# Expert slots of a two-layer mixture-of-experts kernel: gate and up products taken with the weights as the stationary operand

## The chip, the cores and the metric

One core of a Trainium2 chip runs the whole program. The metric is the device time of one execution, in microseconds; lower is better.

## The reference, cut to what matters

Two layers work on x of 16 x 256 tokens with 128 features. Each layer is: normalise and modulate, attention, residual, normalise and modulate, mixture of experts, residual. Only the mixture of experts is touched here. For each token one expert is chosen by the largest router logit; its feed-forward is added to that of a shared expert. Layer 0 (8 experts, hidden width 256) and layer 1 (7 experts, one of the 8 router outputs standing for "none", hidden width 512):

```
h = silu(x_ @ gate[e].T) * (x_ @ up[e].T)          # layer 0, e = argmax of the logits
y = h @ down[e].T                                  # plus the shared expert, same form
hid = (x @ up_w[e]) * silu(x @ gate_w[e])          # layer 1
routed = hid @ down_w[e]                           # 0 where the chosen index is 7
out = ALPHA * top1_val * routed + shared
```

All matrices are fp32.

## The kernel before, in words

The kernel keeps X (features on the partitions, tokens along the row) in SBUF and runs the stages one after the other. In the mixture stage (function `moe`, one on each engine) the tokens are sorted by expert: VectorE works out a place for each token, GpSimd scatters 32 tiles of 128 token rows to the HBM tensor `sorted_rows` (L1458), meanwhile TensorE does the shared expert (L534, L536, L543). Every expert's run of rows is padded to a multiple of 128, so that 39 slots of 128 rows (SLOTS) hold all tokens, each slot of one expert. `eid` holds for each slot the first column of its expert in the weight tensors.

The slots are a software pipeline over k, 39 in each layer:

- SyncE, `tiles` (L259 to L268): waits for all scatters (L261), then fetches slot k's rows, 128 rows of 130 floats, into a ring of 12 places (L268). From k = 12 on it waits for the slot 12 back to be turned, weighted and sent.
- TensorE, loop at L609: `gate_up(k)` (L578, L582), then the register load `first_column(k + 1)` (L564, 4 bytes of `eid` into a TensorE register), `turn(k + 2)` (L571, transpose of the rows), `turn_hidden(k - 1)` (L591, 2 transposes in layer 0, 4 in layer 1), `sum_down(k - 2)` (L600, 2 or 4 products into one bank). In `gate_up` the token block is stationary and the expert's weights are the moving operand, 256 or 512 columns, read from the SBUF copies of all experts at a column held in a register. The product has tokens on the partitions and so has to be turned before `sum_down`.
- ScalarE: `copy_x` (L881) takes the turned rows from PSUM, `silu` (L888) the gate, `weight` (L895) scales the finished slot into `slot_out`.
- VectorE: `gate_hidden` (L1272) multiplies the silu of gate by up, `copy_hidden` (L1280) takes the turned product from PSUM.
- GpSimd: `send` (L1464) scatters the slot's rows to the HBM tensor `token_rows`.

Each engine carries out its list in order, with semaphores between them. After the slots SyncE (`returned`) waits for the sends (12 waits, L275) and fetches the rows back in 8 transfers (L277); TensorE turns them (L628) and VectorE adds them to X (L1157). In layer 0 SyncE also fetches layer 1's up weights, 2 MB, right behind its last slot transfer (L282).

Every fp32 product is two passes, so L578 and L582 appear as x2 for each slot, and L600 as x4 (layer 0) or x8 (layer 1); the transposes are one pass each.

Of the kernel before, what the change touches and what calls it, by code (L numbers as in the profile page):

```python
# [40 lines left out]
def adaln_kernel(nc, a):  # L41
    ctx = ExitStack()
    with ctx:
# [86 lines left out]
        pw = sb("pw", [P, 2, 4, 3 * P])  # L130
        zb = sb("zb", [P, 2 * HEADS1 * DEPTH])
# [51 lines left out]
        slot_sems = {n: sem("r_" + n) for n in ("xt_even", "xt_odd", "eid", "xk", "xf", "gate", "up", "silu", "hidden", "ht", "hf", "down", "y")}  # L183
        r_load, r_sent = [sem(f"r_load{n}") for n in range(RING)], [sem(f"r_sent{n}") for n in range(RING)]
        for l in range(2):
            RS[l].update(slot_sems, load=r_load, sent=r_sent)
# [28 lines left out]
        def of_slot(l, k):  # L215

            return 16 * (l * LOADS[k % RING] + k // RING + 1)

# [3 lines left out]
        def _(sp):  # L222
# [36 lines left out]
            def tiles(l):  # L259
                q = RS[l]  # L260
                sp.wait_ge(q["dispatched"], 16 * TILES)  # L261
                for k in range(SLOTS):
# [5 lines left out]
                    sp.dma_start(slot_in[:, r, :], sorted_rows[l][k * P:(k + 1) * P, :]).then_inc(q["load"][r], 16)  # L268

# [23 lines left out]
        def _(pe):  # L293
# [210 lines left out]
            def moe(c):  # L504
                E, NH, HID, l = c["E"], c["NH"], c["HID"], c["l"]
                up, gate, down, q = c["up"], c["gate"], c["down"], RS[c["l"]]
                up_f = up.rearrange("p e h -> p (e h)")
                gate_f = gate.rearrange("p e h -> p (e h)")
# [76 lines left out]
                def turn_hidden(k):  # L585
                    b = k % 2
                    pe.wait_ge(q["hidden"], l * SLOTS + k + 1)
                    if k >= 2:
                        pe.wait_ge(q["hf"], l * SLOTS + k - 1)
                    for n in range(NH):  # L590
                        m = nc.tensor.transpose(PS[:, 4 + b, n * P:(n + 1) * P], rsb[:, b, n * P:(n + 1) * P], ident[:, :])  # L591
                    m.then_inc(q["ht"], 1)
# [153 lines left out]
        def _(act):  # L746
# [113 lines left out]
            def moe(c):  # L860
# [39 lines left out]
                for k in range(SLOTS + 2):  # L900
                    if k < SLOTS:
                        silu(k)
                    if k + 2 < SLOTS:
                        copy_x(k + 2)
# [650 lines left out]
```

## Time and profile before

| | |
|---|---|
| three runs | 1098.90, 1098.04, 1094.33 us, median 1098.04 |
| profiled execution | 1097.04 us, its span 1095.3 us |
| mean granted TensorE clock | 0.942 |
| TensorE busy | 89% of the span; VectorE 58%, ScalarE 50%, GpSimd 41% |
| slots of layer 0 | from about 605 to 675 us of the span |
| slots of layer 1 | from about 950 to 1080 us of the span |

Times in the rows are us from the start of the span, durations in us unless marked ns. PE is TensorE's matrix multiply, PEld its weight load (which runs beside it), PEldq its sequencer's register work, SPq SyncE's issuing of DMAs. A busy PE is a modelled figure: matmuls are pipelined, and the distance between two starts says more than one duration. A granted clock of 1.00 is 2.4 GHz, 0.50 is 1.2 GHz.

### The profile page before, as it was taken

Reading aid. Unit: us, or ns where it says so; the run is one execution under the profiler, and the core shown is the slowest. Engines: PE = TensorE matmul, PEld = TensorE weight load, DVE = VectorE, ACT = ScalarE, POOL = GpSimd, SP = SyncE. Lnnn points to the kernel's source line nnn. Section 1 sums busy time; section 2 is a strip of 40 time slices with the busy share of each in tenths; the row PEclk is TensorE's granted clock in tenths of the full one; section 3 lists DMA queues with packets and bytes.
Section 4 is the critical chain, followed back from the end, with each engine's and each line's share of the span. In section 5 each row is a group of like instructions: output and inputs, shape, how many; then the busy total and the mean of one; then the engine's idle time right before and its main releaser. Section 6 shows DMA issues by size and latency. Waiting matters only on the chain.

```text
span 1095.3 us, 20328 instructions
## 1 busy us (share of the span) xinstructions
PE 976.8 (89%) x6976; PEld 586.4 (54%) x6976; DVE 632.1 (58%) x2018; ACT 547.5 (50%) x1080; POOL 450.0 (41%) x681
## 2 busy tenths in 40 slices
PE   7778999999986989699889997799997999999995
PEld 4356666666662332244444796356654644366664
DVE  2558888888833789622454343667763633343443
ACT  4605666666666545544622563557775422234331
POOL 1116667766740799200037354035541073023221
PEclk9859999999998998899989998889998899999998
DMA  6500000000002000300001335000000012011105
GB/s 215 193 0 2 2 3 2 3 2 3 2 2 86 1 0 1 153 1 0 1 24 52 78 82 181 8 1 2 1 2 1 1 51 57 0 38 44 43 28 165
DMA packets 31873, 41.91 MB, mean 38 GB/s; under 512 B 6880, under 2 KB 26720, under 8 KB 30912
## 3 DMA queue, kind: packets, MB, share of 16 engines
q1 hardware_dynamic: 27232, 31.26, 9.2%
q0 software_dynamic: 4544, 9.38, 2.6%
q8 instruction: 58, 0.95, 0.4%
q14 instruction: 39, 0.32, 0.1%
HBM read 29.16 MB, written 16.66 MB: 42 GB/s over the span
## 4 chain that ended last, share of the span: by engine, by line
PE 46%; ACT 3%; POOL 3%; DVE 3%; issue 3%; DMA 2%; SPq 0%; DVEq 0%; POOLq 0%
PE PS L578 5%; PE PS L600 5%; PE PS L582 5%; PE PS L534 3%; POOL sorted_rows L1458 3%; PE PS L495 3%; PE PS L536 3%; PE PS L543 3%; PE PS L500 3%; PE PS L591 2%; PE PS L301 2%; PE PS L682 2%; PE PS L701 2%; PE PS L669 2%; PE PS L712 2%
## 5 line engine op out<-in xcount | busy, mean ns | idle before, releaser
L804 ACT ACTIVATE pw<-PS 128x384 f32<-128x384 f32 x256 | 111.7, 488 | 79.1 <-PE PS L415 77.0
L1401 POOL TENSOR_SCALAR_AFFINE_SELECT pw<-pw 128x256 f32<-128x256 f32 x256 | 104.2, 431 | 96.2 <-ACT pw L804 94.3
L1035 DVE CUSTOM_DVE_ANT_0 PS<-PS,above 128x256 f32<-128x256 f32 x256 | 115.3, 450 | 47.2 <-PE PS L390 45.3
L1464 POOL DMA_INDIRECT token_rows<-xnb,slot_in x78 | 74.5, 955 | 161.4 <-ACT xnb L895 161.4
L393 PE MATMUL PS<-kf,qm 32*128 32x256 f32 x512 | 96.4, 454 | 13.2 <-DVE mx L1037 8.0
L1272 DVE TENSOR_TENSOR rsb<-sqb,PS 128x256 f32<-128x256 f32 (+1 forms) x78 | 43.3, 555 | 112.4 <-ACT sqb L888 99.0
L1451 POOL TENSOR_TENSOR XS<-XS,N 128x512 f32<-128x512 f32 x64 | 80.1, 1290 | 28.1 <-DVE N L1108 24.4
L1423 POOL TENSOR_SCALAR_AFFINE_SELECT pw<-pw 128x256 f32<-128x256 f32 x128 | 55.7, 469 | 71.9 <-ACT pw L925 71.9
L1037 DVE CUSTOM_DVE_ANT_0 PS<-PS,above 128x128 f32<-128x128 f32 x256 | 84.4, 330 | 0.0
L1410 POOL TENSOR_SCALAR qm<-qs,qmask 128x256 f32<-128x256 f32 x64 | 60.0, 939 | 56.1 <-ACT kf L790 56.1
L418 PE MATMUL PS<-qm,kf 32*128 32x256 f32 x512 | 82.8, 400 | 0.0
L1458 POOL DMA_INDIRECT sorted_rows<-H,pos x32 | 30.8, 964 | 126.1 <-DVE pos L1253 116.7
L877 ACT ACTIVATE sqb<-PS 128x512 f32<-128x512 f32 x48 | 28.7, 597 | 96.7 <-PE PS L534 96.7
L1010 DVE TENSOR_TENSOR xnb<-PS,rsb 128x512 f32<-128x512 f32 x56 | 38.7, 691 | 65.0 <-ACT rsb L770 45.0
L1183 DVE TENSOR_TENSOR rsb<-sqb,PS 128x512 f32<-128x512 f32 x48 | 32.8, 686 | 68.9 <-PE PS L536 68.9
L483 PE MATMUL PS<-N,wxs 128*128 128x512 f32 x112 | 63.3, 663 | 6.1 <-DVE N L1117 3.3
L846 ACT ACTIVATE PS<-PS,cols 128x512 f32<-128x512 f32 x64 | 42.4, 662 | 41.7 <-DVE N L1117 22.8
L925 ACT ACTIVATE pw<-PS 128x768 f32<-128x768 f32 x64 | 48.4, 809 | 23.4 <-PE PS L685 23.4
L895 ACT ACTIVATE xnb<-PS,slot_in 128x128 f32<-128x128 f32 x78 | 28.6, 367 | 59.8 <-PE PS L600 59.8
L310 PE MATMUL PS<-sqb,meanm 128*128 128x512 f32 x112 | 57.8, 604 | 0.6 <-ACT sqb L759 0.5
L759 ACT ACTIVATE sqb<-PS 128x512 f32<-128x512 f32 x56 | 33.1, 593 | 49.6 <-PE PS L301 47.3
L435 PE MATMUL PS<-pw,region 128*32 128x256 f32 (+1 forms) x1024 | 54.9, 332 | 1.0 <-POOL pw L1401 1.0
(206 smaller groups left out, 2382.8 us busy)
## 6 DMA issues: line engine op xcount, KB each, us to landing
sorted_rows<-empty_rows_dram SPq DMA_DIRECT2D x2, 2535.0 KB, 14.9
slot_in<-sorted_rows SPq DMA_DIRECT2D x78, 65.0 KB, 1.9
N<-token_rows SPq DMA_DIRECT2D x16, 256.0 KB, 4.9
X<-xT_dram SPq DMA_DIRECT2D x4, 512.0 KB, 6.9
ATT<-gate_dram SPq DMA_DIRECT2D x1, 2048.0 KB, 7.7
XS<-down_dram SPq DMA_DIRECT2D x1, 2048.0 KB, 12.3
H<-up_dram SPq DMA_DIRECT2D x1, 2048.0 KB, 8.3
out_dram<-X SPq DMA_DIRECT2D x8, 256.0 KB, 3.3
```

The lines of the kernel that those rows point to most:

```text
L310: nc.tensor.matmul(PS[:, LN_PSV + k % 2, :], meanm[:, :], sqb[:, k % 4, :], start=True, stop=True).then_inc(ln_var, 1)
L393: m = nc.tensor.matmul(PS[:, bank, 0:SEQ], qm[r, b % 3, g, P:SEQ], kf[r, b % 3, :], start=True, stop=True)
L418: m = nc.tensor.matmul(PS[:, bank, 0:SEQ], kf[r, b % 3, 0:P], qm[r, b % 3, g, :], start=False, stop=True, skip_group_check=True)
L483: nc.tensor.matmul(PS[:, k, :], wxs[:, :], V[:, s], start=False, stop=True, skip_group_check=True).then_inc(i_p, 1)
L804: nc.scalar.activation(pw[:, w % 2, j + n, :], PS[:, A_PST + (2 * v + n) % 3, 0:3 * P], ACT.Exp).then_inc(a_p, 1)
L1035: nc.vector.tensor_tensor_reduce(x[:, 0:SEQ], x[:, 0:SEQ], above[:, :], 1.0, -3e38, ALU.add, ALU.max, mx[:, 1, j, g:g + 1])
L1037: nc.vector.tensor_tensor_reduce(x[:, SEQ:SEQ + P], x[:, SEQ:SEQ + P], above[:, P:SEQ], 1.0, -3e38, ALU.add, ALU.max, mx[:, 0, j, g:g + 1] ...
L1401: m = nc.gpsimd.affine_select(x[:, :, SEQ * k:SEQ * k + P], x[:, :, SEQ * k:SEQ * k + P], [[0, 2], [1, P]], ALU.is_ge, 0.0, base=0, channe ...
L1410: nc.gpsimd.tensor_scalar(qm[:, b % 3, g, :], qs[:, b % 2, :], qmask[:, g:g + 1], None, ALU.mult).then_inc(a_q, 1)
L1451: nc.gpsimd.tensor_tensor(XS[:, s], XS[:, s], V[:, s], ALU.add).then_inc(i_x, 1)
L1458: nc.gpsimd.indirect_dma_start(sorted_rows[l][:, :], bass.IndirectOffsetOnAxis(pos[:, n:n + 1], 0), rows[l][:, n, :], None).then_inc(q["di ...
L1464: nc.gpsimd.indirect_dma_start(token_rows[l][:, :], bass.IndirectOffsetOnAxis(slot_in[:, r, D:D + 1].bitcast(mybir.dt.int32), 0), slot_out ...
```

## The change

In the slots, `gate_up` takes the weights as the stationary operand, 128 columns at a time, and the block of 128 tokens as the moving operand. The product comes out with the hidden units on the partitions, as `sum_down` wants it: `turn_hidden`, `copy_hidden` and their semaphores are gone, and the loop on TensorE is one step shorter. Each slot's gate and up weights (2 x 128 KB in layer 0, 2 x 256 KB in layer 1) no longer come from the resident copies: SyncE loads the slot's column from `eid` into a register of its own and transfers both blocks from HBM to one of two fixed places for each. The resident copies stay, for the shared expert. `copy_x` moves from ScalarE to VectorE.

```diff
+        wgate, wup = [pw[:, :, :, :].rearrange("p w u t -> p (w u t)")[:, 2 * FF * n:2 * FF * (n + 1)]
+                      .rearrange("p (b h) -> p b h", b=2) for n in range(2)]
...
+        def of_weights(l, k):
+            return 16 * (l * ((SLOTS + 1 - k % 2) // 2) + k // 2 + 1)
...
             def tiles(l):
                 q = RS[l]
-                sp.wait_ge(q["dispatched"], 16 * TILES)
-                for k in range(SLOTS):
+                HID, cap = MOE[l]["HID"], MOE[l]["cap"]
+                gate_f, up_f = [a[f"{n}{l}"].rearrange("p e h -> p (e h)") for n in ("gate", "up")]
+
+                def rows_in(k):
                     r = k % RING
                     if k >= RING:
                         sp.wait_ge(q["xk"], l * SLOTS + k - RING + 1)
                         sp.wait_ge(q["y"], l * SLOTS + k - RING + 1)
                         sp.wait_ge(q["sent"][r], of_slot(l, k - RING))
                     sp.dma_start(slot_in[:, r, :], sorted_rows[l][k * P:(k + 1) * P, :]).then_inc(q["load"][r], 16)
+
+                def weights_in(k):
+                    e = sp.value_load(eid[0:1, k:k + 1], min_val=0, max_val=cap * HID)
+                    if k >= 2:
+                        sp.wait_ge(q["gate"], l * SLOTS + k - 1)
+                    sp.dma_start(wgate[:, k % 2, 0:HID], gate_f[:, bass.ds(e, HID)]).then_inc(q["wgate"][k % 2], 16)
+                    if k >= 2:
+                        sp.wait_ge(q["up"], l * SLOTS + k - 1)
+                    sp.dma_start(wup[:, k % 2, 0:HID], up_f[:, bass.ds(e, HID)]).then_inc(q["wup"][k % 2], 16)
+
+                sp.wait_ge(q["eid"], l + 1)
+                for k in range(2):
+                    weights_in(k)
+                sp.wait_ge(q["dispatched"], 16 * TILES)
+                for k in range(OUTS):
+                    rows_in(k)
+                for k in range(SLOTS):
+                    if k + 2 < SLOTS:
+                        weights_in(k + 2)
+                    if k + OUTS < SLOTS:
+                        rows_in(k + OUTS)
...
-                def gate_up(k, e):
+                def gate_up(k):
                     b = k % 2
                     pe.wait_ge(q["xf"], l * SLOTS + k + 1)
+                    pe.wait_ge(q["wgate"][b], of_weights(l, k))
                     if k >= 2:
                         pe.wait_ge(q["silu"], l * SLOTS + k - 1)
-                    nc.tensor.matmul(PS[:, b, 0:HID], xnb[:, b, 0:P], gate_f[:, bass.ds(e, HID)],
-                                     start=True, stop=True).then_inc(q["gate"], 1)
+                    for n in range(NH):
+                        m = nc.tensor.matmul(PS[:, b, n * P:(n + 1) * P], wgate[:, b, n * P:(n + 1) * P], xnb[:, b, 0:P],
+                                             start=True, stop=True)
+                    m.then_inc(q["gate"], 1)
+                    pe.wait_ge(q["wup"][b], of_weights(l, k))
                     if k >= 2:
                         pe.wait_ge(q["hidden"], l * SLOTS + k - 1)
-                    nc.tensor.matmul(PS[:, 2 + b, 0:HID], xnb[:, b, 0:P], up_f[:, bass.ds(e, HID)],
-                                     start=True, stop=True).then_inc(q["up"], 1)
+                    for n in range(NH):
+                        m = nc.tensor.matmul(PS[:, 2 + b, n * P:(n + 1) * P], wup[:, b, n * P:(n + 1) * P], xnb[:, b, 0:P],
+                                             start=True, stop=True)
+                    m.then_inc(q["up"], 1)
...
                 def sum_down(k, e):
                     b = k % 2
-                    pe.wait_ge(q["hf"], l * SLOTS + k + 1)
+                    pe.wait_ge(q["hidden"], l * SLOTS + k + 1)
                     if k:
                         pe.wait_ge(q["y"], l * SLOTS + k)
                     for n in range(NH):
-                        m = nc.tensor.matmul(PS[:, 6, 0:D], rsb[:, 2 + b, n * P:(n + 1) * P],
+                        m = nc.tensor.matmul(PS[:, 6, 0:D], rsb[:, b, n * P:(n + 1) * P],
                                              down_f[:, bass.ds(e + n * D, D)], start=(n == 0), stop=(n == NH - 1))
...
-                for k in range(SLOTS + 2):
+                for k in range(SLOTS + 1):
                     if k < SLOTS:
-                        gate_up(k, columns[k])
+                        gate_up(k)
                     if k + 1 < SLOTS:
                         columns[k + 1] = first_column(k + 1)
                     if k + 2 < SLOTS:
                         turn(k + 2)
-                    if 1 <= k <= SLOTS:
-                        turn_hidden(k - 1)
-                    if k >= 2:
-                        sum_down(k - 2, columns[k - 2])
+                    if k:
+                        sum_down(k - 1, columns[k - 1])
...
+                copy_x(0)
+                copy_x(1)
+                for k in range(SLOTS):
+                    gate_hidden(k)
+                    if k + 2 < SLOTS:
+                        copy_x(k + 2)
```

The last lines are VectorE's loop after the change; ScalarE's keeps `silu(k)` and `weight(k - 1)`. SyncE's loop issues three transfers for each slot in place of one, and the slots' rows run 8 ahead in place of 12.

## Rows read from the trace of the kernel before

**Rows 1.** Page, part 1: busy time, share of the span, instructions of each engine.
```profile
PE 976.8 (89%) x6976; PEld 586.4 (54%) x6976; DVE 632.1 (58%) x2018; ACT 547.5 (50%) x1080; POOL 450.0 (41%) x681
```
**Rows 2.** Windows: stretch, then busy PE, PEld, DVE, ACT, POOL; clock, DMA share, GB/s.
```profile
612.00:640.00 28.00, 28.00 (x190) 25.41 (x189) 12.97 (x35) 17.47 (x51) 16.27 (x17) 1.00 0.28 75
1000.00:1060.00 60.00, 60.00 (x326) 40.90 (x325) 24.50 (x38) 23.59 (x57) 18.09 (x19) 1.00 0.15 40
```
**Rows 3.** Chain of waits, one slot of layer 0: start, us, what.
```profile
641.64 0.43 PE PS L578 x2
642.08 0.43 PE PS L582 x2
642.51 0.11 PE PS L571
642.62 0.22 PE PS L591 x2
642.84 0.45 PE PS L600 x4
```
**Rows 4.** Chain of waits, one slot of layer 1.
```profile
1000.03 0.44 PE PS L591 x4
1000.47 0.89 PE PS L600 x8
1001.36 0.86 PE PS L578 x2
1002.22 0.86 PE PS L582 x2
1003.08 0.11 PE PS L571
```
**Rows 5.** Groups of instructions between 1000 and 1060 us, layer 1's slots.
```profile
L600 PEld LDWEIGHTS PS<-XS,rsb 128*128 128x128 f32 x152 | 18.5, 192 | 0.0
L1280 DVE COPY rsb<-PS 128x512 f32<-128x512 f32 x19 | 13.0, 684 | 0.0
```
**Rows 6.** SyncE: timeline from 603.5 us; L268's issues (min/median/max ns); DMA to landing.
```profile
603.59 5.55 SPq L268 DMA_DIRECT2D slot_in<-sorted_rows  x12
L268 SPq DMA_DIRECT2D slot_in<-sorted_rows x78: 319/320/1319, 603.6 to 1045.4; - x78
w<-w_dram SPq DMA_DIRECT2D x2, 256.0 KB, 2.9
wctx<-wctx_dram SPq DMA_DIRECT2D x1, 64.0 KB, 1.9
```
**Rows 7.** Timeline, start of layer 1's slots: start, us, engine, line [idle before].
```profile
948.52 0.88 DVE L1157 SCALAR_TENSOR_TENSOR X<-PS,gab,X 128x256 f32<-128x256 f32 x2 [1.22 <-PE PS L543]
950.19 0.14 PEld L571 LDWEIGHTS PS<-ident,slot_in 128*128 128x128 f32 x1 [2.54 <-issue]
950.56 0.28 ACT L881 ACTIVATE xnb<-PS 128x128 f32<-128x128 f32 x1 [4.28 <-PE PS L571]
950.95 0.14 PEld L571 LDWEIGHTS PS<-ident,slot_in 128*128 128x128 f32 x1 [0.62 <-issue]
```
**Rows 8.** L578's register instructions (min/median/max ns).
```profile
L578 PEldq FUSED_REGOPS  x78: 37/44/46, 606.2 to 1068.8; - x78
```
**Rows 9.** Ends of both slot stages: last up product, last send, SyncE's next issue.
```profile
669.69 0.59 PE L582 MATMUL PS<-region,xnb 128*128 x2
674.27 2.24 DMA token_rows<-xnb,slot_in
676.69 5.71 SPq L277 DMA_DIRECT2D N<-token_rows  x8
1071.43 1.02 PE L582 MATMUL PS<-H,xnb 128*128 x2
1078.00 2.22 DMA token_rows<-xnb,slot_in
```
**Rows 10.** L1464, all sends: issue to landing; layer 0's sends as a group.
```profile
DMA to landing us min/median/max: 2.2/2.4/6.7
L1464 POOL DMA_INDIRECT token_rows<-xnb,slot_in x39 | 37.3, 957 | 35.8 <-ACT xnb L895 35.8
```
**Rows 11.** Windows, columns as in rows 2: two stretches in which TensorE waits.
```profile
50.00:60.00 10.00, 5.79 (x28) 4.38 (x30) 4.11 (x24) 0.37 (x2) 3.63 (x4) 0.50 0.00 1
350.00:360.00 10.00, 6.68 (x16) 2.60 (x15) 5.99 (x11) 6.58 (x11) 0.01 (x1) 1.00 0.00 0
```

More of the change, by code:

```diff
@@ L182, in adaln_kernel @@
             "back", "x")} for l in range(2)]
-        slot_sems = {n: sem("r_" + n) for n in ("xt_even", "xt_odd", "eid", "xk", "xf", "gate", "up", "silu", "hidden", "ht", "hf", "down", "y")}
+        slot_sems = {n: sem("r_" + n) for n in ("xt_even", "xt_odd", "eid", "xk", "xf", "gate", "up", "silu", "hidden", "down", "y")}
+        r_wgate, r_wup = [sem(f"r_wgate{n}") for n in range(2)], [sem(f"r_wup{n}") for n in range(2)]
         r_load, r_sent = [sem(f"r_load{n}") for n in range(RING)], [sem(f"r_sent{n}") for n in range(RING)]
         for l in range(2):
-            RS[l].update(slot_sems, load=r_load, sent=r_sent)
+            RS[l].update(slot_sems, load=r_load, sent=r_sent, wgate=r_wgate, wup=r_wup)
         r_rows = [sem(f"r_rows{n}") for n in range(NCH)]
@@ L506, in moe @@
                 up, gate, down, q = c["up"], c["gate"], c["down"], RS[c["l"]]
-                up_f = up.rearrange("p e h -> p (e h)")
-                gate_f = gate.rearrange("p e h -> p (e h)")
                 down_f = (down[:, :, :, :] if l == 0 else down).rearrange("p e j d -> p (e j d)")
@@ L615, in moe @@
                         turn(k + 2)
-                    if 1 <= k <= SLOTS:
-                        turn_hidden(k - 1)
-                    if k >= 2:
-                        sum_down(k - 2, columns[k - 2])
+                    if k:
+                        sum_down(k - 1, columns[k - 1])
             def turn_back(l, k):
@@ L877, in moe @@
                     nc.scalar.activation(sqb[:, j % 2, :], PS[:, j % 2, :], ACT.Silu).then_inc(q["s_silu"], 1)
-                def copy_x(k):
-                    act.wait_ge(q["xk"], l * SLOTS + k + 1)
-                    nc.scalar.activation(xnb[:, k % 2, 0:P], PS[:, 7, 0:P], ACT.Copy).then_inc(q["xf"], 1)
                 def silu(k):
@@ L896, in weight @@
                                          scale=slot_in[:, r, D + 1:D + 2]).then_inc(q["y"], 1)
-                copy_x(0)
-                copy_x(1)
-                for k in range(SLOTS + 2):
+                for k in range(SLOTS + 1):
                     if k < SLOTS:
                         silu(k)
-                    if k + 2 < SLOTS:
-                        copy_x(k + 2)
-                    if k >= 2:
-                        weight(k - 2)
+                    if k:
+                        weight(k - 1)
             nc.scalar.preload_act_table_set(LN_EXP)
@@ L1270, in gate_hidden, with copy_x @@
                     if k >= 2:
-                        dve.wait_ge(q["ht"], l * SLOTS + k - 1)
+                        dve.wait_ge(q["down"], l * SLOTS + k - 1)
                     nc.vector.tensor_tensor(rsb[:, b, 0:HID], sqb[:, b, 0:HID], PS[:, 2 + b, 0:HID],
                                             ALU.mult).then_inc(q["hidden"], 1)
-                def copy_hidden(k):
-                    b = k % 2
-                    dve.wait_ge(q["ht"], l * SLOTS + k + 1)
-                    if k >= 2:
-                        dve.wait_ge(q["down"], l * SLOTS + k - 1)
-                    nc.vector.tensor_copy(rsb[:, 2 + b, 0:HID], PS[:, 4 + b, 0:HID]).then_inc(q["hf"], 1)
-                for k in range(SLOTS + 1):
-                    if k < SLOTS:
-                        gate_hidden(k)
-                    if k:
-                        copy_hidden(k - 1)
+                def copy_x(k):
+                    dve.wait_ge(q["xk"], l * SLOTS + k + 1)
+                    nc.vector.tensor_copy(xnb[:, k % 2, 0:P], PS[:, 7, 0:P]).then_inc(q["xf"], 1)
+                copy_x(0)
[4 more added lines that the diff above has]
+                        copy_x(k + 2)
             def add_routed(l, k):
```

8 lines of the change are left out of this document (1 added, 7 removed).

## The prediction

> **What bounds the kernel now.** I read the page first: TensorE is busy for 89% of the span [rows 1], but that is a mean over many stages, so the two slot stages are read by themselves. The windows inside them [rows 2] show TensorE busy without a break at full clock (28.00 of 28.00 us, 60.00 of 60.00), every other engine under two thirds busy, and the DMA engines at a share of 0.28 and 0.15. The chain of waits consists there of TensorE alone [rows 3, 4], and its pieces are the price list. Layer 0: gate 0.43, up 0.43, turn 0.11, two transposes 0.22, down 0.45, together 1.64 us a slot. Layer 1: 0.86 + 0.86 + 0.11 + 0.44 + 0.89 = 3.16 us a slot. So each TensorE instruction saved in a slot is saved from the time, until something else ends last. SyncE issues one DMA a slot and is idle otherwise; nothing of the old profile warns of it, and it is where the change puts its work.
>
> **TensorE.** New gate and up are of down's kind: a 128x128 fp32 stationary block, 128 columns moving, two passes. Eight such passes take 0.89 us [rows 4], four 0.45 [rows 3]. Layer 1: three times 0.89 + 0.11 = 2.78 in place of 3.16, 0.38 less. Layer 0: three times 0.45 + 0.11 = 1.46 in place of 1.64, 0.18 less. The two transposed steps' waits on VectorE vanish with them. What must hold is that weight loads go beside products: each of down's loads takes 192 ns by itself [rows 5], and yet eight loads and eight passes fit in 0.89 us, 0.11 for a pair. The Trainium skill, page "TensorE: Matmul & The Clock Gate", section "The mechanism", says that a weight load overlaps a running product only where the two use different row groups. By that rule the pair would cost load plus pass; the rows of down contradict it for just this shape.
>
> **VectorE and ScalarE.** VectorE loses a copy of 256 or 512 columns (0.68 us for 512 [rows 5]) and takes one of 128, surely less; ScalarE loses one. Both were covered by TensorE and have more room now. I cost them at nothing in the steady state. GpSimd needs 0.96 us a send [rows 10] against at least 1.46 a slot: covered.
>
> **Layer 1's sum.** Up to the last up product 37 slots' transposes go (37 x 0.44 = 16.3), 78 products grow by 0.03 (2.3), and one more down stands ahead of it, since the lag is a step shorter (0.9): -13.1. The tail: before, 5.7 us from the end of the last up product (1071.43 + 0.86) to the last send's issue at 1078.00 [rows 9]. After: product on VectorE 0.69, down 0.89, weighting 0.37, four hand-offs of about 0.15: 2.6. So -3.1. Layer 1 together: -16, if SyncE and the DMAs keep up.
>
> **Do they in layer 1?** Gate's place for slot k+2 is free when gate(k) ends, and is needed when gate(k+2) starts, two slots less one gate later: 5.56 - 0.89 = 4.7 us. A 256 KB transfer lands 2.9 us after its issue [rows 6]; with hand-offs 3.2. There is 1.5 us of room. Data: two blocks of 256 KB and the rows come to some 640 KB in 2.8 us, 230 GB/s; the 256 KB landing 1.0 us later than a 64 KB one (2.9 against 1.9 [rows 6]) speaks for 190 KB in 1 us for a transfer by itself. This is no end of the engines' rate, as two are in flight, but it is why late weights stay among the rivals.
>
> **SyncE, the disputed term.** Its list for each slot is now: register load, wait, gate DMA, wait, up DMA, up to three waits, rows DMA. All of it is serial. Priced by rows:
> - Register load: no row shows it on SyncE. On TensorE one stands between the end of VectorE's last shared addition (948.52 + 0.88 = 949.40) and the first transpose's load at 950.19: 0.79 us, where a plain hand-off (ScalarE's copy ends 950.84, next load 950.95) takes 0.11 [rows 7]. So 0.68 for load, its register arithmetic and two passed waits. The lower bound is 0 (if SyncE goes on to its waits while the load is under way), since from there on nothing on TensorE shows it; upper 0.8, all of that gap. I take 0.68, the only direct reading.
> - Three DMA issues: twelve back to back take 5.55, 0.46 each; one by itself 0.32 [rows 6]. The first after the register load at 0.36, the others 0.47: 1.30. Bounds 0.96 and 1.41.
> - Register arithmetic for two addresses: 0.044 for a matmul's [rows 8]; a DMA's may need several. I take 0.09, bounds 0.04 and 0.35.
> - Five passed waits: 12 of them, with the hand-off, fit between the last landing (674.27 + 2.24 = 676.51) and 676.69 [rows 9], so 0.02 each: 0.10.
>
> Sum S = 2.2 us a slot; bounds 1.1 to 2.7, or 1.8 to 2.5 with the register load at 0.68. In layer 1 that is under 2.78, and its steps fit between up(k)'s end and gate(k+1)'s (1.9 us): cost nothing. In layer 0 it is over TensorE's 1.46 and over today's 1.64: **SyncE becomes layer 0's bound**.
>
> **Layer 0's sum.** Weights 0 and 1 go out before the scatters end. From 603.59 eight row transfers take 3.7 us, a register load follows, so gate DMA 2 goes out at 608.0. DMA 38 goes out 36 slots later, 79.2 us, less six slots at the end that have no rows DMA (2.8): 684.4. It lands after 2.3 (between 64 KB's 1.9 and 256 KB's 2.9 [rows 6]; this is an estimate), up's block 0.4 later, up ends 0.5 after that: 687.7. Tail: 0.42 VectorE, 0.45 down, 0.37 weighting, hand-offs 0.6: last send at 689.6, where it was 674.27 [rows 9]. That is +15.3. Behind it: layer 1's up weights (2 MB) are now issued some 2 us before TensorE's last slot, no longer 15 us before the last send, so they are still moving when the last sends go. A send lands after 2.4 us as a rule and after 6.7 at worst [rows 10]; between 0 and 4.3, I take 1. Layer 0: +16.
>
> **Total:** +16 - 16 = 0 against the profiled execution of 1097.04 (span 1095.3 and 1.7 around it). The median of the three runs lies 1.0 higher. Forecast 1098, no change, from two opposite terms of 1.5% each. A measurement of this kernel can tell about 0.5%, 5.5 us, from no change. Each 0.1 us of S is 3.6 us of time, so 0.15 either way leaves that band.
>
> **Rivals.**
> 1. *SyncE is cheaper, and the change wins.* The load may run beside the waits, or isolated issues may cost 0.32 each. With no blocking load S = 1.5; then the loop through the two places binds: gate 0.45, hand-offs 0.2, landing 2.3 to 2.9, for two slots, so 1.5 to 1.8 a slot. At 1.6 layer 0's last send goes at 670.3, 4 us earlier, less the 1: -3, total -19, 1079. With S = 1.9 layer 0 gains 11 on my sum: 1087. For: issues get cheaper when spaced. Against: 0.68 in [rows 7] was waited for in full. Chance 0.28.
> 2. *SyncE is dearer, and the change loses.* One mechanism: address arithmetic and issue at their upper ends, S = 2.6. Layer 0 grows by 14 more: 1112. The turning point is S = 2.35. Beyond S = 2.8 layer 1 loses also. For: a DMA from HBM at an address from a register is nowhere in the trace. Chance 0.26.
> 3. *The clock falls in layer 0.* TensorE would be 1.46 of 2.2 us busy, 66%. At 350 to 360 us it is 67% busy at clock 1.00, but at 50 to 60 us 58% busy at 0.50 [rows 11], and the stage begins after an idle gap. At 0.50 a slot costs 2.92, more than S: for half of the slots +13, 1111; for all +26, 1124. The Trainium skill, same page, section "HAM oscillation", tells of a kernel whose short bursts of products each waited for a DMA and fell to the low clock in every wait. Chance 0.12.
> 4. *Layer 1's weights come late*: landing 5 us or more after gate(k) in place of 3.2. At 0.2 us a slot its gain halves: 1106. Chance 0.04. *Weight loads do not go beside products*: 16 passes at 0.11 + 0.19 take 4.8 for gate and up in layer 1 in place of 1.8, over 100 us in all. Chance 0.01.
>
> **How the numbers follow.** My case has 0.29, all within 0.5%. Rival 1 is faster by over 0.5% nearly wholly: 0.29 with a little of the forecast's lower edge. Rivals 2 to 4 are slower nearly wholly: 0.42. Range: down to 1080 (below it lies a third of rival 1, 0.09) and up to 1120 (above it SyncE beyond 2.8 and a clock low throughout, 0.10). The forecast's own range is 1092 to 1104.
>
> **What would show it.** In layer 1: TensorE without a break, 2.78 a slot in the chain, stage shorter by 16. In layer 0: the chain goes through SyncE's issues, TensorE waits for the weight DMAs, SyncE's period is 2.2, TensorE about 66% busy at clock 1.00. A period of 1.6 with waits on landings shows rival 1; a period of 2.6 with SyncE never waiting, rival 2; a granted clock under 0.9 from 612 on, rival 3; TensorE gaps in layer 1, rival 4. The forecast is wrong if S is off by more than 0.15, in either direction, while layer 1 may still be right.

## The result: slower by 0.6%, and the profile after

| | before | after |
|---|---|---|
| median of nine runs each | 1095.19 us | 1102.72 us |
| lowest to highest | 1091.98 to 1099.95 | 1098.85 to 1108.64 |
| profiled execution, its span | 1097.04, 1095.3 | 1103.41, 1101.3 |
| mean granted clock | 0.942 | 0.943 |
| slots of layer 0, first turn of a block to SyncE's first return transfer | 71.3 | 88.5 |
| slots of layer 1, the same | 130.2 | 114.5 |

The ratio is 1.0062, with a 95% interval from 1.0033 to 1.0091: slower, by a little more than this kernel's measurement can tell from nothing. The forecast was 1098 and no change.

Both halves of the forecast are in the trace: layer 0 became longer (+17.2 in this pair of profiles), layer 1 shorter (-15.7). Of the 6.0 us by which the two spans differ these two make only 1.5; 5.4 lie ahead of layer 0's slots, whose first turn comes at 610.8 in place of 605.4, in parts that the change does not touch. The account of the sum below returns to them. The windows in the two slot stages of the kernel after, with busy PE, PEld, DVE, ACT and POOL, the granted clock, the DMA engines' share and GB/s, answer to [rows 2]:

```profile
612.00:640.00 28.00, 24.66 (x173) 21.07 (x172) 8.39 (x27) 9.71 (x26) 10.83 (x12) 1.00 0.63 177
640.00:680.00 40.00, 34.97 (x236) 29.07 (x235) 11.44 (x36) 13.61 (x37) 17.41 (x19) 1.00 0.63 180
980.00:1020.00 40.00, 40.00 (x360) 39.93 (x359) 13.11 (x30) 13.51 (x28) 13.45 (x14) 1.00 0.79 236
```

In layer 1 TensorE is busy throughout, as before; in layer 0 it no longer is, and the clock stays at 1.00 all the same. The modelled busy share (24.66 of 28) hides how much it waits. The count of passes says it better: 173 in 28 us, where a slot has 13 (four each of gate, up and down, one transpose), so 13.3 slots, 2.1 us each. At 1.45 us of work a slot that is 69% of the stretch; the forecast had 66%.

One slot of layer 1 in the chain of waits (start, us, what), the answer to [rows 4]:

```profile
1000.54 0.89 PE PS L609 x8
1001.43 0.89 PE PS L616 x8
1002.33 0.11 PE PS L600
1002.43 0.89 PE PS L626 x8
1003.33 0.89 PE PS L609 x8
```

Each slot's gate, up, turn and down start 2.79 us after those of the slot before, where 3.16 was the old distance and 2.78 the forecast. Eight weight loads and eight passes fit in 0.89 for gate and up too.

In layer 0 the place to look is SyncE. Its timeline in the kernel after (start, us, line; L277 is a slot's rows, L284 gate, L287 up):

```profile
609.01 3.66 SPq L277 DMA_DIRECT2D slot_in<-sorted_rows  x8
613.42 0.34 SPq L284 DMA_DIRECT2D pw<-gate_dram  x1
613.87 0.37 SPq L287 DMA_DIRECT2D pw<-up_dram  x1
614.28 0.43 SPq L277 DMA_DIRECT2D slot_in<-sorted_rows  x1
615.44 0.33 SPq L284 DMA_DIRECT2D pw<-gate_dram  x1
...
617.48 0.33 SPq L284 DMA_DIRECT2D pw<-gate_dram  x1
...
625.58 1.16 SPq L284 DMA_DIRECT2D pw<-gate_dram  x1
...
640.04 1.59 SPq L277 DMA_DIRECT2D slot_in<-sorted_rows  x1
...
689.27 0.52 SPq L284 DMA_DIRECT2D pw<-gate_dram  x1
689.89 0.39 SPq L287 DMA_DIRECT2D pw<-up_dram  x1
```

The period is 2.02, then 2.04 (615.44 - 613.42, 617.48 - 615.44), and 2.03 in the mean of the steps after them in which nothing is late. The blank piece is always the same: a rows issue ends at 614.71 and the next gate issue starts at 615.44, 0.73 us later. What fills it is in the register instructions of the two lines (min/median/max ns):

```profile
L281 SPq TENSOR_LOAD <-eid x78: 262/272/477, 568.2 to 1072.6; - x78
L281 SPq FUSED_REGOPS  x78: 147/147/186, 568.7 to 1073.0; - x78
L281 SPq SEQ_ASSERT  x78: 18/18/37, 568.9 to 1073.2; - x78
L284 SPq ALU_OP  x78: 32/33/51, 569.0 to 1074.2; - x78
```

The first three are the load of the slot's column, its register arithmetic and the check of its range (TENSOR_LOAD, FUSED_REGOPS, SEQ_ASSERT); the fourth is the arithmetic for gate's address, and a move of 29 ns follows it for each of the two transfers. Now and then one issue by itself takes 0.7 to 1.6 us (five times in 37 slots). From gate's transfer of slot 2 (613.42) to that of slot 38 (689.27) are 75.85 us: 31 steps with a rows issue in them take 67.48, the last five, without one, 8.37. 31 times 2.03 would be 62.9; of the other 4.6 the five long issues make 3.4 (what each took over its usual 0.33 to 0.4), SyncE's waits most of the rest. That SyncE is bound by its own list, and not held by TensorE, is in its waits from 612 to 689 us (for whom, total, times, longest):

```profile
SPq L284 <- PE PS L609: 0.8, 3, 0.5
SPq L277 <- PE PS L600: 0.6, 1, 0.6
SPq L287 <- PE PS L616: 0.2, 1, 0.2
```

1.6 us of waiting in 77. TensorE's side shows the same: a transfer raises its semaphore in 16 steps, whose times the trace has, and 24 of the 37 gate products from slot 2 on start within 0.12 us of the last step of their weights' transfer. That step comes 2.2 us after the issue in the median. The end of the stage, in the chain of waits, answers to [rows 9]:

```profile
693.30 0.45 PE PS L616 x4
693.74 0.47 PE PS L626 x4
...
694.24 0.38 ACT xnb L915
...
694.85 0.72 PE PS L626 x4
...
695.60 0.38 ACT xnb L915
695.97 0.27 issue
696.24 2.85 DMA token_rows<-xnb,slot_in
```

The last up product ends 4.5 us after the last gate transfer was issued (693.74 - 689.27), forecast 3.2; the last send goes 2.5 later, forecast 1.9; it lands in 2.85, where it was 2.24. Between the last up product and that send stand two rounds of down (L626) and of the weighting (L915): slot 37's, then slot 38's, whose down waits until slot 37's weighting has emptied the one bank that down writes.

### The profile page after: what moved, and what is told of

The parts are those of the page before. It is cut to its first block, busy times and chain, and to the rows that moved or that the text cites. A ratio compares the mean times of both kernels' runs of the same rounds, so it can differ in the third digit from the quotient of the medians.

```text
span 1101.3 us, 21430 instructions
## 1 busy us (share of the span) xinstructions
PE 972.8 (88%) x7366; PEld 614.5 (56%) x7366; DVE 612.0 (56%) x2018; ACT 526.1 (48%) x1002; POOL 451.4 (41%) x681
## 4 chain that ended last, share of the span: by engine, by line
PE 42%; issue 4%; ACT 3%; POOL 3%; DVE 3%; DMA 3%; SPq 2%; DVEq 0%; POOLq 0%
PE PS L626 4%; PE PS L616 4%; PE PS L609 4%; PE PS L526 3%; PE PS L563 3%; POOL sorted_rows L1473 3%; PE PS L565 3%; PE PS L572 3%; PE PS L531 2%; PE PS L332 2%; PE PS L706 2%; PE PS L736 2%; PE PS L693 2%; PE PS L725 2%; PE PS L341 2%
## 5 line engine op out<-in xcount | busy, mean ns | idle before, releaser
L1051 DVE CUSTOM_DVE_ANT_0 PS<-PS,above 128x256 f32<-128x256 f32 x256 | 115.4, 451 | 48.0 <-PE PS L421 46.3
L424 PE MATMUL PS<-kf,qm 32*128 32x256 f32 x512 | 97.5, 459 | 13.3 <-DVE mx L1053 8.0
L901 ACT ACTIVATE sqb<-PS 128x512 f32<-128x512 f32 x48 | 28.7, 597 | 97.7 <-PE PS L563 97.7
L915 ACT ACTIVATE xnb<-PS,slot_in 128x128 f32<-128x128 f32 x78 | 28.7, 368 | 92.4 <-PE PS L626 92.4
L609 PE MATMUL PS<-xnb,pw 128*128 128x128 f32 x468 | 66.9, 279 | 5.2 <-issue 3.9
L616 PE MATMUL PS<-xnb,pw 128*128 128x128 f32 x468 | 66.4, 278 | 2.3 <-DMA pw<-up_dram 2.3
L609 PEld LDWEIGHTS PS<-xnb,pw 128*128 128x128 f32 x468 | 58.4, 191 | 7.6 <-issue 4.2
L616 PEld LDWEIGHTS PS<-xnb,pw 128*128 128x128 f32 x468 | 58.4, 192 | 3.5 <-DMA pw<-up_dram 3.1
```

The costliest lines, as they stand in the source:

```text
L424: m = nc.tensor.matmul(PS[:, bank, 0:SEQ], qm[r, b % 3, g, P:SEQ], kf[r, b % 3, :], start=True, stop=True)
L609: m = nc.tensor.matmul(PS[:, b, n * P:(n + 1) * P], wgate[:, b, n * P:(n + 1) * P], xnb[:, b, 0:P], start=True, stop=True)
L616: m = nc.tensor.matmul(PS[:, 2 + b, n * P:(n + 1) * P], wup[:, b, n * P:(n + 1) * P], xnb[:, b, 0:P], start=True, stop=True)
L1051: nc.vector.tensor_tensor_reduce(x[:, 0:SEQ], x[:, 0:SEQ], above[:, :], 1.0, -3e38, ALU.add, ALU.max, mx[:, 1, j, g:g + 1])
```

## The experiments

Each run below stands beside runs of the kernel before on the same chip. Lengths of a slot stage run from the first turn of a block to SyncE's first return transfer. The first question was whether the two halves are what the profile pair says, and whether they add up.

**The two kernels again, and each layer by itself.** In the two mixed kernels one layer's loops on all engines have the form of before, the other's that of after:

```diff
+NEW = (False, True)        # only_layer1; only_layer0 has (True, False)
...
+                if not NEW[l]:
+                    sp.wait_ge(q["dispatched"], 16 * TILES)
+                    for k in range(SLOTS):
+                        rows_in(k)
+                    return
```

and so on TensorE, ScalarE and VectorE.

> The kernel before, unchanged, as a check of how far two programs with the same work differ. Two theories of why the change came out slower although layer 0's slots lost 16 us and layer 1's won 16 as forecast: (A) the 5.4 us by which the changed kernel's first scatter starts later (567.3 against 561.8) is what executions vary by in stages that the change doesn't touch; (B) it belongs to the changed program. A: ratio to before within 0.3% of 1, first scatter anywhere between 560 and 568. B: the same ratio, and the first scatter again near 562, within 1 us.

> The changed kernel again. Layer 0's stage from the first row transfer to the last send's issue 86 us where it is 70.7 before, layer 1's from the first turn to the last send 112 where it is 127.8: these two cancel within 1 us. A (upstream varies by execution): the first scatter starts anywhere between 560 and 568, and the ratio comes nearer to 1.000 than the 1.0062 measured. B (upstream belongs to the program): first scatter near 567 again, ratio about 1.006.

> Layer 0's slots as before, layer 1's slots in the new form with SyncE's weight transfers. By my account of the slots layer 1 gains 16 us and layer 0 nothing is lost: ratio 0.985 (1079). If the stages ahead of the slots are longer by 5 in any program that has the new code (B), 0.990. If layer 1's gain needed layer 0's change, no gain at all.

> Layer 0's slots in the new form, layer 1's as before. Layer 0's slots lose 16: ratio 1.015 (1111). With B 1.019 to 1.020. SyncE's period in layer 0 2.03 us with some stalls, mean 2.1.

| | ratio to before, 95% interval | layer 0's slots | layer 1's slots |
|---|---|---|---|
| before again | 0.9994, 0.9968 to 1.0020 | 71.2 | 130.2 |
| after again | 1.0046, 1.0029 to 1.0063 | 88.6 | 115.7 |
| only layer 1 new | 0.9878, 0.9841 to 0.9916 | 71.3 | 114.5 |
| only layer 0 new | 1.0172, 1.0143 to 1.0201 | 88.9 | 130.3 |

So the change is two independent ones: layer 0's is worth +18.9 us (0.0172 x 1097.9), layer 1's -13.4, and their sum, +5.5, fits the loss measured beside them (0.46%, 5.1 us) and the first one (0.62%, 6.8 us). The intervals of the two are some 3 to 4 us wide to either side, and the forecast's +16 and -16 lie within them. Layer 1's form by itself beats both kernels.

**SyncE's list, one item at a time.** `no_register_load` uses the constant 0 in place of the slot's column (every slot then takes the first expert's gate and up); `one_register_load` loads a register once in a layer and takes every slot's address from it; `rows_by_scalar_queue` gives the rows' transfers to ScalarE from the ninth slot on; `one_transfer_three_places` lays gate and up side by side in HBM and fetches them in one transfer to one of three places, three slots ahead.

```diff
 no_register_load
-                    e = sp.value_load(eid[0:1, k:k + 1], min_val=0, max_val=cap * HID)
+                    e = 0
 one_register_load
+                    if not held:
+                        held.append(sp.value_load(eid[0:1, k:k + 1], min_val=0, max_val=cap * HID))
+                    e = held[0]
 rows_by_scalar_queue: SyncE's loop loses rows_in(k + OUTS), ScalarE has after its weight(k - 1)
...
+                        act.dma_start(slot_in[:, r, :], sorted_rows[l][n * P:(n + 1) * P, :]).then_inc(q["load"][r], 16)
 one_transfer_three_places
+                    if k >= 3:
+                        sp.wait_ge(q["up"], l * SLOTS + k - 2)
+                    sp.dma_start(wgu[:, k % 3, 0:2 * HID], gu_f[:, bass.ds(e * 2, 2 * HID)]).then_inc(q["wgu"][k % 3], 16)
```

> The changed kernel with the column of the slots' weights fixed at 0, so SyncE has no register load and no address from a register (every slot then uses expert 0's gate and up; the transfers are as many and as large). My account: SyncE's base period in layer 0, 2.03 us, loses the register load, about 0.68, and is 1.35, under TensorE's 1.46; then the two places bind: (0.45 + 0.2 + landing 2.3 to 2.9)/2 = 1.5 to 1.8 a slot, layer 0's stage 11 to 20 us shorter than in the changed kernel (ratio to the kernel before 0.99 to 0.995). Rival (SyncE's period is made by the DMA engines' backlog or by the issues alone, and the load runs beside): the period stays at 2.0, ratio 1.005. Layer 1 in both the same as in the changed kernel.

> As the changed kernel, but SyncE loads its register once in each layer and keeps it, so the address still comes from a register and only the loads are gone (all slots use the first slot's expert for gate and up). If the load is the 0.68 and the address arithmetic little, layer 0's period is within 0.1 of the one without any register; if the arithmetic is dear (my rival 2), it stays 0.2 to 0.5 above it.

> Gate and up of an expert side by side in HBM (a layout made ahead of the launch), one transfer for both in each slot, three places of 2 x hidden width in place of two and two. SyncE's period in layer 0 falls by one issue, 0.43, and one wait: 1.58. Three places leave room for a landing of 3 us (three slots less gate and up: 3.5 us at 1.46). So layer 0 at 1.6 a slot, 16 us shorter than in the changed kernel, about as before the change; layer 1 unchanged: ratio 0.983 to 0.988 (1080). Rival (backlog of the DMA engines is what makes layer 0's period): same bytes in fewer transfers, 2.0 a slot, ratio 1.005.

> The changed kernel, with the rows' transfers from the ninth slot on issued by ScalarE, so SyncE's list loses one issue and three waits: period 2.03 - 0.43 - 0.06 = 1.55; the two places then bind at 1.5 to 1.8. ScalarE has 0.38 + 0.37 + 0.35 of work in 1.5. Layer 0 10 to 18 us shorter than in the changed kernel, layer 1 the same: ratio 0.988 to 0.995. Rival (backlog of the DMA engines): unchanged, 1.005.

| | ratio to before, 95% interval | layer 0's slots | layer 1's slots |
|---|---|---|---|
| no register load | 0.9954, 0.9930 to 0.9979 | 81.8 | 113.9 |
| one register load | one run, 1090.92 us | 78.0 | 115.4 |
| rows by ScalarE's queue | 0.9968, 0.9946 to 0.9990 | 83.0 | 116.3 |
| one transfer, three places | 0.9899, 0.9869 to 0.9930 | 72.7 | 115.4 |

All four act where SyncE was said to bind, in layer 0, and leave layer 1 within 2 us of the kernel after. They gained less than expected in two cases: 7 us without the load, where 11 to 20 were expected, and 6 with the rows on ScalarE, expected 10 to 18 (against 89.0, the mean of the kernel after on other chips); and the merged transfer's ratio is just above its expected 0.983 to 0.988. The register load's price stands in SyncE's timeline of the kernel without it:

```profile
613.03 0.43 SPq L277 DMA_DIRECT2D slot_in<-sorted_rows  x1
613.63 0.33 SPq L284 DMA_DIRECT2D pw<-gate_dram  x1
...
614.73 0.34 SPq L277 DMA_DIRECT2D slot_in<-sorted_rows  x1
615.69 0.33 SPq L284 DMA_DIRECT2D pw<-gate_dram  x1
```

From the rows issue's end to the next gate issue are now 0.17 us (613.46 to 613.63) where there was 0.73: the load and the register instructions behind it took 0.56, of which the load itself is 0.27, and SyncE issued nothing meanwhile. With one load kept in a register the same step is 0.16 (the third row is the address arithmetic in that kernel):

```profile
617.48 0.37 SPq L277 DMA_DIRECT2D slot_in<-sorted_rows  x1
618.01 1.47 SPq L288 DMA_DIRECT2D pw<-gate_dram  x1
L288 SPq ALU_OP  x2: 37/46/55, 564.6 to 885.6; - x2
```

The arithmetic, too, ran only once in a layer there, so this kernel does not price it; a move of 29 ns for each address stayed and cannot be seen in the step. In the kernel after the arithmetic's own row has 33 ns, within the 0.56. The second row shows one of the long issues. Other steps in these two timelines are longer (615.07 to 615.69): with a list of 1.5 us SyncE arrives before the place is free, and the loop through two places binds, as rival 1 had it. Its waits without the load, from 612 to 670 us, show it, where the kernel after has 0.8 up to 689:

```profile
SPq L284 <- PE PS L609: 16.3, 30, 1.0
```

Gate's weights also landed later there, 2.8 us after the issue in the median, which makes that loop longer. Merging two transfers leaves the load in and takes out an issue and a wait; its timeline has a steady 1.57, near the 1.45 that TensorE needs there:

```profile
614.12 0.34 SPq L283 DMA_DIRECT2D pw<-gu_dram  x1
...
615.68 0.34 SPq L283 DMA_DIRECT2D pw<-gu_dram  x1
...
617.24 0.34 SPq L283 DMA_DIRECT2D pw<-gu_dram  x1
...
620.98 1.53 SPq L276 DMA_DIRECT2D slot_in<-sorted_rows  x1
623.27 0.34 SPq L283 DMA_DIRECT2D pw<-gu_dram  x1
```

The long issue at 620.98 delays the next weights by 1.2 us (2.75 from 620.52 to 623.27, not 1.57). TensorE did not wait for those, though: they landed 0.75 us before their gate product started. Layer 0 is back at its old length and no shorter, though its TensorE work fell by 0.19 a slot.

**What is under SyncE.** Two more kernels: no weight transfers at all (gate and up stationary from fixed columns of the resident copies, so every slot takes the same expert there, and SyncE only fetches rows), and the merged transfer with the rows given to ScalarE, so that SyncE's list is about 1.1 us by the prices above. The first runs of them are from another chip, on which all programs took some 40 us more; the second from a chip like the first.

```diff
 no_weight_transfers
-                        m = nc.tensor.matmul(PS[:, b, n * P:(n + 1) * P], wgate[:, b, n * P:(n + 1) * P], xnb[:, b, 0:P],
+                        m = nc.tensor.matmul(PS[:, b, n * P:(n + 1) * P], gate_f[:, n * P:(n + 1) * P], xnb[:, b, 0:P],
 one_transfer_rows_by_scalar: one_transfer_three_places with the edit of rows_by_scalar_queue
```

> The new order on TensorE, VectorE and ScalarE with no weight transfers at all: gate and up are taken from the resident copies at column 0 (every slot uses expert 0's gate and up), SyncE only fetches rows, 12 ahead, as before the change. By my account TensorE alone then sets both stages: 1.46 a slot in layer 0, 2.78 in layer 1; layer 0's stage (first row transfer to first return transfer) 73 - 7 - 1 = 65 to 66 us, layer 1's turn to last send 112. Ratio 0.978 to 0.981. If something else than SyncE's list and the transfers made layer 0 longer (hand-offs of the shorter pipeline, copy_x on VectorE), layer 0 stays above 70.

> One transfer for gate and up with three places, and the rows' transfers from the ninth slot on issued by ScalarE: SyncE's list is register load 0.58, one issue 0.36, two waits: about 1.1 a slot, under TensorE's 1.46. Layer 0 at 1.46 to 1.55 a slot if the DMA engines carry 385 KB in that time (260 GB/s): stage 67 to 70 us where one transfer alone gave 74.5; ratio 0.982 to 0.986. Rival: the DMA engines (share 0.8 at 1.6 a slot) are the next bound, stage 73 or more.

> Layer 0 as before, layer 1 in the new form, once more, for a narrower interval: slots say 0.9856, the first interval was 0.984 to 0.992. Expect 0.984 to 0.990.

> The changed kernel a third time, for the clock ahead of the slots. In both its profiles the low clock after the idle stretch at 443 us and again after 467 us lasts 3 us longer than in the seven profiles of kernels without it, which costs 1.6 us each. If that is a property of the program, it is there again; if it is chance, one profile in three or so has it.

> The kernel before, for its profile beside the others of this call on the same chip. First turn to last send 68.9 us in layer 0 and 127.8 in layer 1, as in its two profiles so far.

> The changed kernel. Slots: 85 to 86 and 112 to 113 us, together 1 us more than before. If the rest of its loss (3 to 5 us) belongs to the program, the ratio is again 1.0045 to 1.0065 and the low clock after 443 and after 467 us lasts 10 and 7 us where the kernel before has 7 and 3.5. If it is chance of the clock, one of the two is as before and the ratio is nearer 1.002.

> The new order on the engines without weight transfers, on a chip where the earlier one was disturbed (its stages ahead of the slots were 20 us longer in every program, and ScalarE began late in every other slot, at 1.72 us a slot). If that was the chip: 1.46 a slot, first turn to last send 62 us in layer 0, 111.5 in layer 1, ratio 0.977 to 0.980. If the shorter pipeline itself has a hand-off that is too long, 1.72 again, 70 us, ratio 0.985 to 0.988, and then the forecast's floor of 1.46 for layer 0 was wrong too.

> One transfer for gate and up, three places, rows by ScalarE, for the same reason again. SyncE's list is 1.1 a slot. If the DMA engines keep up, 1.5 a slot, 63 to 65 us in layer 0, ratio 0.980 to 0.984; if their backlog binds, 68 to 70 us, ratio 0.986 to 0.990.

| | ratio to before, 95% interval | layer 0's slots | layer 1's slots |
|---|---|---|---|
| *the slower chip (before 1135.61 us)* | | | |
| no weight transfers | 0.9901, 0.9866 to 0.9936 | 73.0 | 113.7 |
| one transfer, rows by ScalarE | 0.9930, 0.9902 to 0.9958 | 74.7 | 113.8 |
| only layer 1 new, again | 0.9895, 0.9863 to 0.9927 | 71.3 | 113.8 |
| after, third | one run, 1145.19 us | 87.4 | 115.2 |
| *a chip like the first (before 1094.92 us)* | | | |
| before, third | one run, 1099.26 us | 69.7 | 130.2 |
| after, fourth | 1.0052, 1.0032 to 1.0072 | 89.8 | 116.8 |
| no weight transfers, again | 0.9804, 0.9771 to 0.9837 | 61.8 | 115.4 |
| one transfer, rows by ScalarE, again | 0.9908, 0.9882 to 0.9934 | 73.0 | 115.3 |

The windows of layer 0 in three kernels, columns as above: no weight transfers (second time); then one transfer with three places; then that with the rows by ScalarE (second time):

```profile
612.00:640.00 28.00, 28.00 (x253) 27.97 (x253) 12.16 (x40) 14.30 (x39) 18.05 (x19) 1.00 0.34 92
```
```profile
612.00:640.00 28.00, 25.12 (x206) 23.58 (x206) 9.54 (x32) 11.96 (x32) 14.49 (x16) 1.00 0.77 225
```
```profile
612.00:640.00 28.00, 26.16 (x215) 25.25 (x215) 10.18 (x33) 12.01 (x32) 14.89 (x16) 0.97 0.78 221
```

Without the weight transfers TensorE makes 253 passes in 28 us without a break, 19.5 slots at 1.44. That is the floor of this form of the products; the stage is 7.9 us under the old one on the same chip (61.8 against 69.7 in its one profile there; the other two profiles of the kernel before have 71.2 and 71.3). Taking the stationary operand from the resident copies at each slot's own column, which would keep the right experts without a transfer, was not tried. With the weights streamed it makes 206, and 215 where SyncE has almost nothing to do: a slot of 1.7 to 1.77. So behind SyncE there is a second limit of about the old slot length, and it is not SyncE's list. In the last kernel SyncE waits for TensorE for 21.1 us of 58, and none of its issues is long (its waits from 612 to 670 us; its issues in both layers, min/median/max ns):

```profile
SPq L283 <- PE PS L609: 21.1, 35, 1.9
L283 SPq DMA_DIRECT2D pw<-gu_dram x78: 332/333/363, 566.8 to 1054.8; - x78
```

What TensorE waits for is in its chain:

```profile
620.76 0.42 DVE rsb L1289
621.18 0.21 DVE xnb L1295
621.39 1.07 issue
622.46 0.68 PE PS L603 x4
```

TensorE's products run for some slots at 1.45, then it stands at the gate product (L603) until 1.07 us after the last engine it waited for was done; the only other thing that this product waits for is its weights. The DMA engines are at a share of 0.78 there, against 0.28 before. The semaphore steps confirm it: these weights were issued at 617.66 and landed at 622.37, 4.7 us later, and the product started 0.09 after that. Over the layer the merged transfers landed 3.5 us after their issue in the median (3.3 with the rows on SyncE), and 15 of 36 gate products started within 0.12 us of such a landing. Late weights are thus what is left, and since this kernel has no long issue of weights, it is their landing that makes them late. Whether memory or the DMA engines make it slow was not separated.

On the slower chip ScalarE began its weighting later in every other slot of the kernel without transfers (1.72 a slot), so its layer 0 gained nothing there. In the kernel after the extra time lay in the two shared-expert stages: the first starts of L563 span 67.9 and 104.8 us, where they span 46.2 and 82.3 in its first profile. Why is open. The order of after (one run there) and before, and layer 1's gain, were the same on both chips.

Of the expectations for these runs, the first of the kernel without transfers missed (73.0 and 0.9901, expected 65 to 66 and 0.978 to 0.981); on the chip like the first its ratio came at the edge (0.9804, expected 0.977 to 0.980). SyncE's shortest list gave 74.7 and 73.0, as its rival had it (73 or more), not the 67 to 70 first expected.

## Why the prediction was wrong by a little

The mechanism was right and the cancelling of the two layers was not: both sums were too favourable. The terms that were mis-sized are the ends of the two stages (the step from the last weights' issue to the last up product in layer 0, and the tail behind it in both layers) and, in part, what sets the clock and the landings at a stage's start. By term:

- **TensorE's prices, right.** 2.79 a slot in layer 1 (forecast 2.78); 1.45 in layer 0 where nothing holds it (1.46). Weight loads go beside products for gate and up as for down, eight loads and eight passes in 0.89. The Trainium skill, page "TensorE: Matmul & The Clock Gate", section "The mechanism", has the rule in two forms: its list, which the prediction told, lets a load overlap only where the row groups differ, and a sentence above it adds a load into the background weight buffer. The runs speak against the first form, since here all loads and products use the whole array; which buffer a load goes to no run shows.
- **VectorE and ScalarE at nothing, right in the steady state** of the chips like the first: the chain of layer 1's slots has TensorE alone. Their part in the tails is told below.
- **SyncE binds layer 0 and not layer 1, right.** It waits 1.6 us in 77 in layer 0; removing the load, an issue or a transfer each shortens layer 0 by 6 to 16 us and layer 1 by at most 2.
- **S = 2.2, right only in sum.** The list by itself measured 2.03: load with its register and address arithmetic 0.56 (taken 0.68 and 0.09), issues and waits 1.47 (taken 1.40). The load need not have been read from a gap: the trace of the kernel before has TensorE's own, 302 ns in the median, with 151 and 18 behind it for the arithmetic and the check, 0.47 together.

```profile
L564 PEldq TENSOR_LOAD <-eid x78: 295/302/502, 604.2 to 1065.9; - x78
```

By the forecast's own 3.6 us for 0.1 that would have won 6 us. What took most of it back was no item of the list: long issues and waits, 4.6 us over 31 slots, so that the mean was 2.18. [Rows 6] had shown one issue of 1319 ns beside a median of 320, and I did not price it.
- **Layer 0's sum, the step that failed.** +16 forecast, +17.2 in the first pair of profiles, +18.2 as a mean of three against three, +18.9 by the times of the kernel with this layer alone. The steady part came out right (75.85 against 79.2 - 2.8 = 76.4, though five steps have no rows issue, not six). The end did not. The last up product ended 1.3 later behind its transfer's issue than taken (1.4 and 0.4 in the second and fourth profiles). Its own weights were in time, gate's 2.29 us after their issue, as taken; TensorE was late, because slot 37's gate weights had landed 2.97 us after theirs, where 2.2 was the median (3.62 and 2.81 in those two profiles). Then the tail had a step missing: it was summed as one product on VectorE, down and weighting, but slot 37's down and weighting stand between, for the one bank. That cost 0.6 here, and the tail has the same length within 0.1 us in all profiles of the kernel after. Of the 1 us given to the last send's landing, 0.6 was used in this profile.
- **Layer 1's sum, the other half.** -16 forecast; -15.7 in the first pair, -14.5 in the mean of three, -13.4 by times. Its tail lacks the same step: from the start of the last up product to the last send's issue are 4.5 us in each profile, 3.5 by the forecast. Part of the other difference is chance of the clock: where the stage begins at the low clock, as in the fourth profile of after,

```profile
974.13 0.95 PE PS L609 x8
975.09 1.65 PE PS L616 x8
```

eight passes cost 1.65 in place of 0.89. In after's first profile both stand at 0.95 and 0.91, which flattered it. Sends were slower too, without setting the time: layer 1's land in 3.7 us in the median, where it was 2.2, while layer 0's land in 2.3 to 3.0 over the three profiles (2.4 to 2.6 before). Layer 1's row in the first profile of after:

```profile
DMA to landing us min/median/max: 3.0/3.7/4.0
```

The Trainium skill, page "DMA: Bandwidth & Descriptors", section "Latency and other measured facts", says that a transfer's fixed cost grows with the load on HBM; this row agrees, though no run here separates the memory from the DMA engines.
- **Total, the step on which the call hung.** +16 and -16 were called 0. With errors of up to 3 us in each, both to the bad side, the sum was +5.5, just at the 0.5% line that the forecast had named itself. It could be known that a difference of two terms of 1.5%, each with such an error, was nearly as likely outside the band as in it; it could not be known on which side, except that the terms left out (long issues, late landings, slot 37's down in both tails) all point to slower. That the total came within 5 us is in part luck: the list was taken 0.17 a slot too dear, and the long issues made up for it.
- **Rivals.** 1, SyncE cheaper through a load that runs beside the waits: refuted, the load and its register instructions held SyncE for all their 0.56. 2, dearer at S = 2.6: refuted in size (2.03), right in sign. 3, the clock falls in layer 0: refuted, 1.00 in both windows. 4, late weights in layer 1: hardly, TensorE waits for up's transfer 0.2 to 0.3 us in one place; in after's fourth profile four slots are longer by 0.1 to 0.6, 1.2 us together, which is part of that stage's 116.8.

The profile stages' means give +18.2 - 14.5 = +3.7, the times +5.5. The rest lies outside the slots, in parts that the change does not touch: the first turn comes at 610.0 in the mean of three, where it is 606.7 before, and the stretch between the layers' slots is 1.5 shorter. Two windows show it, in the kernel before and in the kernel after (first profiles, columns as above):

```profile
450.00:460.00 10.00, 10.00 (x24) 4.40 (x23) 3.99 (x7) 8.31 (x16) 0.00 (x0) 0.98 0.89 380
```
```profile
450.00:460.00 10.00, 10.00 (x17) 4.19 (x18) 1.09 (x2) 4.94 (x9) 0.00 (x0) 0.69 0.93 364
```

After an idle gap the clock came back early in one (24 passes) and late in the other (17). The kernel before has the late form too, in its third profile (0.74), and `only_layer0`, `no_register_load` and `rows_by_scalar_queue`, which run the same stages ahead of the slots with the new code behind them, have 1.00 in this window; on the chip of the last runs all four kernels have the late form (0.69 to 0.83). So I take it as chance of the execution. That it has nothing to do with the change was not shown: the kernel after has the late form in all three profiles on such chips (0.69, 0.81, 0.69), and its fourth run came out with the ratio, 1.0052, that was expected if the loss belongs to the program.

## What to carry to other kernels

When a change gives an engine's queue new steps in a loop, write its list for one turn (here: 0.56 for the register load and what goes with it, three issues of 0.41 to 0.45 with their gaps, 0.17 more from the list's end to its next issue) and compare it with the turn of the bounding engine: at 2.79 it was free, at 1.45 it set the time. Make such a change only in the loop that is longer than the list, or shorten the list first: one merged transfer with one more place gave back 16 us. Where the forecast is a difference of two large terms, ask which effects were priced at their undisturbed durations, since those err on one side, and write out the end of a pipeline instruction by instruction: both tails lacked a step.

## What the runs showed of the hardware that was not expected

- A register load from SBUF, with the register arithmetic and range check that follow it, holds SyncE for 0.56 us and is not hidden by waits behind it. The Trainium skill, page "DMA: Bandwidth & Descriptors", section "Latency and other measured facts", gives a floor of about 600 ns for such a load; the trace has 0.27 us in the median for the load alone, so the measurement is under that floor.
- With weights streaming, a single DMA issue can take 0.7 to 1.6 us where 0.33 to 0.44 is the rule, five times in the 37 slots of layer 0, on rows', gate's and up's transfers alike. Four of the five go with a late landing: of a transfer issued up to 2 us before, gate's or up's, 15 of 16 steps had come after 2.1 to 2.2 us, the last only after 3.4 to 4.1, where 2.2 is the median. Why is open.
- The same programs took 40 us more on another chip (before 1135.61 us, not 1095); in the kernel after all of it lay outside the slots.
- One layer's TensorE floor was hidden under two limits in a row: SyncE's list (2.1 a slot), then late weights (1.7 to 1.77), then TensorE (1.44).
